# The experts' weight split moved out of the self-attention stage into 25 periods of the cross-attention

## Chip, cores and metric

One core of one Trainium2 chip runs the whole program. The metric is the device time of one execution in microseconds (us), smaller is better.

## What is computed

One block of a perceiver: 32 batch elements of 64 tokens, width 256, 16 heads of 16. Three layers stand behind one another, each added to its input: cross-attention to a context of 1601 rows per batch element, causal self-attention with a gate for each key, and a mixture of 8 experts of which each token takes two.

```python
x = x + xattn(layernorm(x), ctx, ctx, mask, Wq, bq, Wk, bk, Wv, bv)      # softmax(q k^T / 16) v over 1601 keys
x = x + attn(layernorm(x), ...)                                          # causal, attn * gate[key], then @ Wo
...
for e in range(E):                                                       # E = 8, F = 704
    h1 = x_rep @ w1[e].T
    a, g = jnp.split(h1, 2, axis=-1)
    he = jax.nn.silu(a) * g @ w2[e].T
    out = out + jnp.where((expert_ids == e)[:, None], he, 0)
```

All arrays are float32. The kernel multiplies with float16 pairs: a high part that is the rounded value, and a low part that is what the rounding lost.

## The kernel before

**Stages.** A lead-in (0 to about 74 us: layer norm, queries, keys and values of batch element 0), 31 periods of the cross-attention (about 74 to 1329 us), the self-attention stage, in which the last batch element's cross-attention is finished too (1329 to 1576 us), the router (to 1610 us) and the experts (to 1882 us). There is no scheduler at run time: what each engine does in a period, and in which order, stands in tables of step names written out in the file (`PE_ORDER`, `ACT_ORDER`, `POOL_ORDER`, `DVE_ORDER`, and `SELF_PE` to `SELF_SP` for the self-attention stage). Each engine runs its own list in order and waits on semaphores.

**A period.** In period b the attention of batch element b runs beside the projections of element b+1. On PE (TensorE), `S0`..`S12` are the transposed scores of 13 blocks of 128 keys, `W0`..`W12` the products of weights and values, `K0`..`K7` and `V0`..`V6` the projections of the next element, `M0`..`M15` scores whose maxima are wanted, two matmuls of 402 columns each. On ACT (ScalarE) `E` are two exponentials of 128x1024 (`pT` in float32, `ph` in float16), `KH` writes the high part of a key projection, `CH` that of the context. On POOL (GpSimd) `L` is `low_part`, which subtracts `ph` from `pT`, both in SBUF, into `pl`; `CL` does the same with the context, `ADD` adds a finished pair of elements to `x_all`, in every second period. On DVE (VectorE) `X0`..`X15` is `maxima`: the scores of `M` in PSUM plus the mask `mbias`, reduced to a maximum; `KL` is the low part of a key projection, `VH`, `VL` the two parts of a value projection, `N` the division by the row sums, `MP` the mask for two elements on.

**The banks.** `M(n+1)` writes the two PSUM banks that `X(n)` reads, so it waits for `X(n)`, and since PE runs in order, all of PE's list behind it waits too. `X(n+1)` waits for `M(n+1)`. Between `X(n)` and `X(n+1)` DVE thus has at least the length of an `M` without work of the maxima.

**SP (the DMA queue).** SP issues a period's transfers in this order: the context of b+2 (`cx`), queries (`qst`), twelve transfers of keys of the first half (`kst`, after `KL3`), mask and block queries (`msk`, `qm`), twelve of the second half (after `KL7`), and last the row that holds the maxima (`shift_queries`, `qst<-turned`). `S0` of the next period waits for that last one.

**Weights of the experts.** The 8 experts' weights are 24 pieces of 128x1408 float32. Each is loaded into `w_whole` (step `WL` on SP), its high part is made by ACT (`HI`, an activation with a scale), its low part by DVE (`LW`, a `scalar_tensor_tensor` that reads `w_whole` and the high part, both in SBUF), and both are stored to DRAM (`WS`). All 24 stand between the steps of the self-attention stage. The experts' stage loads them from there after the router.

**Self-attention stage.** `ZS`, `ZE`, `ZL`, `ZW` and `ZN` are the last element's `S`, `E`, `L`, `W` and `N`. `ST`, `N` make the layer norm's scale of a group of tiles (`newton_rsqrt`, some 14 small dependent DVE instructions), `XN` applies it, `X` turns tiles, `Q`, `K`, `V` project, `QH`, `QL`, `KH`, `KL`, `VV` keep them, `MX`, `RM`, `T`, `MC` find the maxima, `S`, `E`, `W`, `O` are the attention, `A`, `AC`, `WO`, `R` the output projection, `NU` and `XU` the next layer norm, `TU`, `CU`, `RT`, `RC` the router's products, `BO` adds a bias on POOL.

Of the kernel before, what the change touches and what calls it, by code (L numbers as in the profile page):

```python
# [137 lines left out]
SELF_PE = steps("ZS0 ZS1 ZS2 ZW0 ZS3 ZS4 ZW1 ZS5 ZW2 ZS6 ZW3 X0 X1 ZW4 ZS7 V0 V1 ZW5 ZS8 Q0 Q1 ZS9 ZW6 ZS10 ZW7 ZW8 V2 "  # L138
# [7 lines left out]
SELF_ACT = steps("ZE0 ZE1 ZE2 ZE3 ZE4 XN0 XN1 XN2 XN3 ZE5 XC0 XC1 XN4 ZE6 ZE7 ZE8 QH0 QH1 ZE9 ZE10 ZE11 ZE12 KH0 XN5 "  # L146
# [6 lines left out]
SELF_POOL = steps("ZL0 ZL1 ZL2 ZL3 ZL4 BO0 ZL5 ZL6 ZL7 ZL8 ZL9 ZL10 ZL11 ZL12 BO1 ZA0 BO2 HG0 BO3 HW0 PR0 HM0 VG0 VG1 "  # L153
                  "VG2 VG3 HG1 HW1 PR1 HM1 VG4 VG5 VG6 VG7")
SELF_DVE = steps("ZN0 ST0 ST1 ST2 ST3 ST4 N0 ST5 ST6 ST7 ST8 ST9 ST10 ST11 ST12 ST13 ST14 N1 VV0 HS0 VV1 HS1 QL0 QL1 "
# [1711 lines left out]
```

## Time and profile before

| | us |
|---|---|
| median of 3 runs | 1889.3 (1888.94 to 1891.74) |
| the profiled execution, its time | 1884.02 |
| its span, first to last instruction | 1882.2 |
| 31 periods of the cross-attention, one | 40.33 mostly, 40.5 on average |
| self-attention stage | 247 |
| router | 34 |
| experts | 272 |

The profiled execution lies 5.3 us under the median. PE is busy 92% of the span, DVE 74%, ACT and POOL 69% each; in the periods of the cross-attention PE is at 98 to 99%, in the self-attention stage at 82%.

### The profile page before, as it was taken

The page shows a single profiled execution, that of the slowest core. Times are in us where ns is not written, and L with a number is a line of the kernel's source. Part 1 is how long each engine was busy: PE and PEld are TensorE (multiplying, and loading weights), DVE is VectorE, ACT ScalarE, POOL GpSimd, SP SyncE. Part 2 cuts the span into 40 slices and gives each one's busy share as a digit, 9 for nine tenths or more (in the row PEclk, how much of TensorE's full clock was granted, in tenths as well). Part 3 has the DMA queues.
Part 4 walks back from the last instruction along what each step waited for, and adds up shares of the span by engine and source line. Part 5 has one row for each costly group of instructions (what it writes and reads, how often), then busy time and mean ns, then how long its engine had stood idle before and what let it go on. Part 6 is the DMA issues. An engine that isn't in the chain of part 4 may idle for free. (4 is left out here: it accounts for less than half of the span.)

```text
span 1882.2 us, 59167 instructions
## 1 busy us (share of the span) xinstructions
PE 1736.2 (92%) x24673; PEld 1146.0 (61%) x24673; DVE 1387.1 (74%) x3579; ACT 1307.0 (69%) x1610; POOL 1293.4 (69%) x669
## 2 busy tenths in 40 slices
PE   6899999999999999999999999999778993699996
PEld 3566666666666666666666666666534672588885
DVE  7788888888888888888888888788766566544443
ACT  5588788888878888878888878888664442233332
POOL 3488888898888888898898888888652100243442
PEclk9999999999999999999999999999898785799998
DMA  8544445444445544445554545554166674688884
GB/s 274 157 119 121 128 113 156 130 127 112 131 117 151 136 129 112 131 117 146 138 132 111 132 117 142 134 138 104 51 215 203 202 236 148 241 248 254 267 245 119
DMA packets 170923, 290.83 MB, mean 155 GB/s; under 512 B 56162, under 2 KB 138466, under 8 KB 170434
## 3 DMA queue, kind: packets, MB, share of 16 engines
q1 hardware_dynamic: 163170, 276.83, 50.6%
q0 software_dynamic: 7488, 10.23, 2.7%
q8 instruction: 196, 3.21, 0.7%
q14 instruction: 69, 0.57, 0.1%
HBM read 169.80 MB, written 33.16 MB: 108 GB/s over the span
## 5 line engine op out<-in xcount | busy, mean ns | idle before, releaser
L420 POOL TENSOR_TENSOR pl<-pT,ph 128x1024 f16<-128x1024 f32 x416 | 881.7, 2132 | 188.4 <-ACT ph L462 188.2
L679 DVE CUSTOM_DVE_ANT_0 junk<-ring,mbias 128x804 bf16<-128x804 f32 x496 | 491.5, 991 | 155.7 <-issue 150.1
L460 ACT ACTIVATE pT<-score,small 128x1024 f32<-128x1024 f32 (+1 forms) x416 | 464.5, 1117 | 68.0 <-PE score L485 34.0
L462 ACT ACTIVATE ph<-score,small 128x1024 f16<-128x1024 f32 (+1 forms) x416 | 464.5, 1117 | 0.0
L883 PE MATMUL ring<-cp,wkp 128*128 128x402 f16 x1536 | 309.0, 338 | 10.2 <-DVE kst L758 3.3
L894 PE MATMUL ring<-wvp,cp 128*128 128x256 f16 (+1 forms) x2496 | 306.3, 274 | 2.9 <-DVE v L664 1.7
L894 PEld LDWEIGHTS ring<-wvp,cp 128*128 128x128 f16 (+1 forms) x2496 | 233.7, 99 | 78.4 <-issue 21.8
L623 POOL TENSOR_TENSOR cp<-cx,cp 128x804 f16<-128x804 f32 x128 | 252.9, 1996 | 21.5 <-ACT cp L792 21.5
L800 ACT ACTIVATE kh<-ring,small 128x402 f16<-128x402 f32 x256 | 155.2, 606 | 154.9 <-PE ring L883 154.9
L908 PE MATMUL ring<-kh,qm 32*128 32x402 f16 x992 | 253.1, 334 | 4.9 <-DVE mx L679 0.3
L507 PE MATMUL o_acc<-v,pl 128*128 128x33 f16 (+1 forms) x3328 | 240.2, 178 | 0.0
L502 PE MATMUL o_acc<-v,ph 128*128 128x66 f16 x2912 | 219.7, 192 | 1.4 <-POOL pl L420 1.2
L883 PEld LDWEIGHTS ring<-cp,wkp 128*128 128x128 f16 x1536 | 131.9, 98 | 134.7 <-DVE v L664 25.8
L502 PEld LDWEIGHTS o_acc<-v,ph 128*128 128x128 f16 x2912 | 179.6, 97 | 54.8 <-issue 41.7
L507 PEld LDWEIGHTS o_acc<-v,pl 128*128 128x128 f16 (+1 forms) x3328 | 211.8, 96 | 1.6 <-issue 0.8
L485 PEld LDWEIGHTS score<-qst,kst 64*128 64x128 f16 x6656 | 156.3, 97 | 49.2 <-issue 1.1
L670 DVE SCALAR_TENSOR_TENSOR kl<-ring,small,kh 128x402 f16<-128x402 f32 x256 | 160.1, 634 | 21.5 <-ACT kh L800 16.9
L481 PE MATMUL score<-delta,mbias 64*128 64x512 bf16 (+1 forms) x832 | 163.3, 389 | 12.8 <-ACT ph L462 5.7
L655 DVE CAST v<-ring 128x512 f16<-128x512 f32 (+1 forms) x217 | 140.3, 652 | 44.7 <-PE ring L894 41.3
L485 PE MATMUL score<-qst,kst 64*128 64x64 f16 x6656 | 167.0, 191 | 0.0
L1488 POOL DMA_INDIRECT acc_d<-ys,to_row x39 | 63.1, 1617 | 144.9 <-DMA acc_d<-ys,to_row 72.1
L1755 PE MATMUL score<-xp,w1p 128*128 128x256 f16 (+1 forms) x1584 | 151.2, 254 | 5.4 <-DMA w1p<-wsp 5.0
(243 smaller groups left out, 2098.5 us busy)
## 6 DMA issues: line engine op xcount, KB each, us to landing
cx<-in_ctxT SPq DMA_DIRECT2D x32, 1601.0 KB, 6.7
w1p<-wsp SPq DMA_DIRECT2D x24, 1408.0 KB, 8.0
kst<-kh SPq DMA_DIRECT2D x256, 100.5 KB, 2.9
...
kst<-kh SPq DMA_DIRECT2D x256, 99.6 KB, 2.5
...
kst<-kl SPq DMA_DIRECT2D x128, 100.5 KB, 2.7
```

The lines of the kernel that those rows point to most:

```text
L420: pool.tensor_tensor(pl[:, u].rearrange("p h q -> p (h q)"), pT[:, u], ph[:, u].rearrange("p h q -> p (h q)"), ALU.subtract).then_inc(pl_r ...
L460: act.activation(pT[0:n, u].rearrange("k (h a q) -> k a h q", a=2, q=S), scored, ACT.Exp, bias=lift[0:n, 0:1], scale=SSCALE)
L462: act.activation(ph[0:n, u].rearrange("k h (a q) -> k a h q", a=2), scored, ACT.Exp, bias=lift[0:n, 0:1], scale=SSCALE).then_inc(exp_done, 1)
L481: pe.matmul(score[0:n, 2 * slot + side, :], mbias[part, j, rows], delta[part, :], start=True, stop=False, skip_group_check=True)
L485: mm = pe.matmul(score[0:n, 2 * slot + side, S * p:S * p + S], kst[j][part, p, rows], qst[part, j, p, :], start=False, stop=True, skip_gro ...
L502: pe.matmul(o_acc[:, at:at + 2 * PW], high, vv.rearrange("k z w -> k (z w)"), start=(kt == 0 and p == 0), stop=last, skip_group_check=True)
L507: mm = pe.matmul(o_acc[:, at:at + PW], low, vv[:, 0, :], start=False, stop=last, skip_group_check=True)
L623: pool.tensor_tensor(cp[:, j, 1, :, chunk(n)], cx[:, :, chunk(n)], cp[:, j, 0, :, chunk(n)], ALU.subtract).then_inc(cl_ready, 1)
L679: dve.tensor_tensor_reduce(junk[:, n % 2], made[:, :, 0:KW], mbias[:, j, 2 * KW * half:2 * KW * half + 2 * KW].rearrange("p (c k) -> p c k ...
L883: mm = pe.matmul(ring[:, bank, 0:KW], wkp[:, z, cc, P * t:P * t + P], cp[:, j, y, cc, chunk(c)], start=(cc == 0 and z == y), stop=(cc == D ...
L894: mm = pe.matmul(ring[0:n, bank, D * half:D * half + D], cp[:, j, z, cc, P * kt:P * kt + n], wvp[:, y, cc, :], start=(cc == 0 and z == y), ...
L908: mm = pe.matmul(to[:, c, 0:KW], qm[rows, j, t], kh[rows, t, chunk(2 * half + c)], start=True, stop=True)
```

## The change

The 24 pieces are split in the cross-attention. Period b (0 to 23) loads piece b and makes its high part on ACT as the last step of `ACT_ORDER`; period b+1 makes the low part on DVE in four slices of 352 columns (`LW0` to `LW3`, each where `DVE_ORDER` names it) and stores both. There is one buffer in place of two, over tiles of the lead-in that are no longer read (`xn`, `pack`, `bv`). The self-attention stage keeps all its other steps, in new orders on all engines, and its small tiles lie elsewhere. No arithmetic is changed.

```diff
+LPARTS = 4
+WSLICE = WP // LPARTS
...
-DVE_ORDER = steps("KL0 N KL1 KL2 VH0 VL0 KL3 X0 KL4 X1 X2 VH1 X3 VL1 X4 X5 KL5 X6 VH2 X7 VL2 X8 X9 KL6 X10 X11 KL7 X12 "
-                  "X13 VH3 X14 VL3 X15 SH VH4 SPR VL4 VH5 VH6 VL5 VL6 MP")
+DVE_ORDER = steps("KL0 N KL1 KL2 VH0 VL0 KL3 LW0 X0 KL4 X1 LW1 X2 VH1 X3 VL1 X4 X5 KL5 X6 VH2 X7 VL2 X8 LW2 X9 KL6 X10 "
+                  "LW3 X11 KL7 X12 X13 VH3 X14 VL3 X15 SH VH4 SPR VL4 VH5 VH6 VL5 VL6 MP")
...
-SELF_DVE = steps("ZN0 ST0 ST1 ST2 ST3 ST4 N0 ST5 ST6 ST7 ST8 ST9 ST10 ST11 ST12 ST13 ST14 N1 VV0 HS0 VV1 HS1 QL0 QL1 "
+SELF_DVE = steps("ST0 ST1 ST2 ST3 N0 ZN0 ST4 ST5 ST6 ST7 ST8 ST9 ST10 ST11 N1 VV0 HS0 VV1 ST12 ST13 HS1 ST14 VV2 QL0 "
...
+                    def load_whole(q):
+
+                        e, k = q // PIECES, q % PIECES
...
+                        after(sp, w_low, LPARTS * q)
+                        if k < DC:
+                            sp.dma_start(w_whole[:], a["w1T"][e, P * k:P * k + P]).then_inc(w_in, 16)
...
+                    def store_parts(q):
+
+                        sp.wait_ge(w_low, LPARTS * q + LPARTS)
+                        sp.dma_start(wsp[q // PIECES, q % PIECES], w_parts[:]).then_inc(w_out, 16)
...
+                        if 1 <= b <= E * PIECES:
+                            store_parts(b - 1)
+                        if b < E * PIECES:
+                            load_whole(b)
                         stack_keys(b + 1, 1 - j, 1)
...
+                            elif kind == "LW" and 1 <= b <= E * PIECES:
+                                cols = slice(WSLICE * n, WSLICE * n + WSLICE)
+                                dve.wait_ge(w_high, b)
+                                dve.scalar_tensor_tensor(w_parts[:, 1, cols], w_whole[:, cols], WSCALE, w_parts[:, 0, cols], ALU.mult, ALU.subtract).then_inc(w_low, 1)
...
+                            elif kind == "HI" and b < E * PIECES:
+                                act.wait_ge(w_in, 16 * (b + 1 + (b + 1) // PIECES))
+                                after(act, w_out, 16 * b)
+                                act.activation(w_parts[:, 0], w_whole[:], ACT.Copy, scale=WSCALE).then_inc(w_high, 1)
...
-                        elif kind == "LW":
-                            j = n % 2
-                            dve.wait_ge(w_high, n + 1)
-                            dve.scalar_tensor_tensor(w_parts[:, j, 1], w_whole[:, j], WSCALE, w_parts[:, j, 0], ALU.mult, ALU.subtract).then_inc(w_low, 1)
...
-                        elif kind == "HI":
```

The piece of DVE's list from `KL3` to `X2` in a period, before (`ISA junk,mx` is the maximum, `ISA mx` the read of its result):

```order
L670 SCALAR_TENSOR_TENSOR kl<-ring,small,kh 128x402
L678 MEMSET small 128x1
L679 ISA junk,mx<-ring,mbias 128x804
L679 ISA mx 128x1
L670 SCALAR_TENSOR_TENSOR kl<-ring,small,kh 128x402
L678 MEMSET small 128x1
L679 ISA junk,mx<-ring,mbias 128x804
L679 ISA mx 128x1
L678 MEMSET small 128x1
L679 ISA junk,mx<-ring,mbias 128x804
```

The same piece now:

```order
L699 SCALAR_TENSOR_TENSOR kl<-ring,small,kh 128x402
L755 SCALAR_TENSOR_TENSOR w_parts<-w_whole,w_parts 128x352
L707 MEMSET small 128x1
L708 ISA junk,mx<-ring,mbias 128x804
L708 ISA mx 128x1
L699 SCALAR_TENSOR_TENSOR kl<-ring,small,kh 128x402
L707 MEMSET small 128x1
L708 ISA junk,mx<-ring,mbias 128x804
L708 ISA mx 128x1
L755 SCALAR_TENSOR_TENSOR w_parts<-w_whole,w_parts 128x352
L707 MEMSET small 128x1
L708 ISA junk,mx<-ring,mbias 128x804
```

`LW0` stands ahead of `X0` and `LW1` ahead of `X2`; in the same way `LW2` stands ahead of `X9` and `LW3` ahead of `X11`. All four read two tiles in SBUF.

SP's list in the middle of a period, before, from the end of the first half's keys:

```order
L548 DMA kst<-kl 32x2x804
L527 DMA msk<-in_mask 64x1601 x2
L532 DMA qm<-qm_d 128x256
L548 DMA kst<-kh 32x2x797 x2
L548 DMA kst<-kl 32x2x797
```

The same place now:

```order
L549 DMA kst<-kl 32x2x804
L528 DMA msk<-in_mask 64x1601 x2
L533 DMA qm<-qm_d 128x256
L572 DMA wsp<-w_parts 128x2816
L562 DMA w_whole<-in_w1T 128x1408
L549 DMA kst<-kh 32x2x797 x2
```

The store of one piece and the load of the next stand between `qm` and the second half's keys; the store waits for `LW3`.

The head of DVE's list in the self-attention stage, before (the first eight rows end the step `ZN0`):

```order
L442 TENSOR_TENSOR osum<-o_acc,rs 64x112
L443 TENSOR_TENSOR o_acc<-o_acc,rs 64x7x16
L442 TENSOR_TENSOR osum<-o_acc,rs 64x112
L443 TENSOR_TENSOR o_acc<-o_acc,rs 64x7x16
L448 TENSOR_TENSOR att<-osum,o_acc 64x7x16
L449 TENSOR_SCALAR att<-o_acc,rs 64x16
L448 TENSOR_TENSOR att<-osum,o_acc 64x7x16
L449 TENSOR_SCALAR att<-o_acc,rs 64x16
L1094 BN_STATS st_x<-x_all 128x6 x5
L1101 BN_AGGR mv_70<-st_x 128x2 x4
```

And now:

```order
L1112 BN_STATS st_x<-x_all 128x6 x4
L1119 BN_AGGR mv_72<-st_x 128x2 x4
L231 TENSOR_SCALAR ln_ve<-mv_72 128x4
L232 TENSOR_SCALAR ln_t<-ln_ve 128x4
L233 TENSOR_SCALAR ln_ve<-ln_ve 128x4
```

The first layer norm's scales (`N0`) no longer stand behind `ZN0`, and on ACT `XN0` now stands behind two steps `ZE` where five stood before.

## Rows read from the trace of the kernel before

**Rows 1.** Busy us by stage (x instructions): PE, PEld, DVE, ACT, POOL; clock, DMA share, GB/s

```profile
164.00:1290.00 1126.00, 1109.71 (x17095) 698.99 (x17095) 923.20 (x2387) 940.07 (x1053) 988.55 (x486) 1.00 0.48 128
1329.00:1576.00 247.00, 201.39 (x2962) 135.23 (x2958) 160.69 (x423) 131.83 (x182) 66.75 (x40) 0.83 0.59 191
```

**Rows 2.** Timeline of one period (start us, us, engine, instruction): DVE, then PE

```profile
931.03 0.64 DVE L670 SCALAR_TENSOR_TENSOR kl<-ring,small,kh 128x402 f16<-128x402 f32 x1
932.46 0.99 DVE L679 CUSTOM_DVE_ANT_0 junk<-ring,mbias 128x804 bf16<-128x804 f32 x1 [0.79 <-issue]
...
934.09 0.99 DVE L679 CUSTOM_DVE_ANT_0 junk<-ring,mbias 128x804 bf16<-128x804 f32 x1
...
935.71 0.99 DVE L679 CUSTOM_DVE_ANT_0 junk<-ring,mbias 128x804 bf16<-128x804 f32 x1 [0.61 <-issue]
...
946.97 0.99 DVE L679 CUSTOM_DVE_ANT_0 junk<-ring,mbias 128x804 bf16<-128x804 f32 x1
...
948.70 0.99 DVE L679 CUSTOM_DVE_ANT_0 junk<-ring,mbias 128x804 bf16<-128x804 f32 x1 [0.73 <-issue]
...
950.31 0.99 DVE L679 CUSTOM_DVE_ANT_0 junk<-ring,mbias 128x804 bf16<-128x804 f32 x1
...
952.01 0.99 DVE L679 CUSTOM_DVE_ANT_0 junk<-ring,mbias 128x804 bf16<-128x804 f32 x1 [0.70 <-issue]
...
933.52 0.51 PE L908 MATMUL ring<-kh,qm 32*128 32x402 f16 x2
```

**Rows 3.** Timeline of POOL in that period, and in one with ADD (first row)

```profile
890.89 4.22 POOL L420 TENSOR_TENSOR pl<-pT,ph 128x1024 f16<-128x1024 f32 x2
...
928.46 4.25 POOL L420 TENSOR_TENSOR pl<-pT,ph 128x1024 f16<-128x1024 f32 x2
...
935.85 4.22 POOL L420 TENSOR_TENSOR pl<-pT,ph 128x1024 f16<-128x1024 f32 x2 [0.63 <-ACT ph L462]
...
945.22 6.33 POOL L420 TENSOR_TENSOR pl<-pT,ph 128x1024 f16<-128x1024 f32 x3
952.45 2.13 POOL L420 TENSOR_TENSOR pl<-pT,ph 128x1024 f16<-128x1024 f32 x1 [0.90 <-ACT ph L462]
```

**Rows 4.** Timeline of POOL and DVE where both ran in SBUF

```profile
1333.80 10.46 POOL L420 TENSOR_TENSOR pl<-pT,ph 128x1024 f16<-128x1024 f32 x5 [5.62 <-ACT ph L462]
...
1342.23 2.05 DVE L239 TENSOR_TENSOR ln_t<-ln_t,ln_ve 128x4 f32<-128x4 f32 x1
...
1453.02 2.35 POOL L1068 TENSOR_TENSOR hd<-hd,lnb 128x1024 f32<-128x1024 f32 x1
...
1453.23 3.63 DVE L1159 SCALAR_TENSOR_TENSOR w_parts<-w_whole,w_parts 128x1408 f16<-128x1408 f32 x1 [0.51 <-ACT w_parts L1247]
```

**Rows 5.** Instructions of the tiles w_parts and ln_t: count, ns min/median/max

```profile
L1247 ACT ACTIVATE w_parts<-w_whole x24: 1360/1368/1389, 1378.5 to 1574.1; 128x1408 f16<-128x1408 f32 x24
L1159 DVE SCALAR_TENSOR_TENSOR w_parts<-w_whole,w_parts x24: 1600/1618/3628, 1382.5 to 1575.5; 128x1408 f16<-128x1408 f32 x24
...
L239 DVE TENSOR_TENSOR ln_t<-ln_t,ln_ve x33: 161/164/2054, 7.4 to 1567.8; 128x4 f32<-128x4 f32 x21, 128x8 f32<-128x8 f32 x9, 128x12 f32<-128x12 f32 x3
```

**Rows 6.** Timeline of ACT at the end of a period

```profile
924.54 0.60 ACT L800 ACTIVATE kh<-ring,small 128x402 f16<-128x402 f32 x1 [4.43 <-PE ring L883]
```

**Rows 7.** Timeline of SP there, and landing of the tile turned

```profile
921.77 0.60 SPq L563 DMA_DIRECT2D qst<-turned  x1
...
DMA to landing us min/median/max: 1.8/1.9/3.4
```

**Rows 8.** PE's waits in the self-attention stage: us in total, times, longest

```profile
PE ring L1366 <- ACT kst L1238: 6.2, 1, 6.2
...
PE ring L1304 <- ACT xn L1197: 3.7, 1, 3.7
...
PE ring L1304 <- DVE klo L1113: 2.3, 1, 2.3
PE o_acc L1349 <- DVE ao L1165: 2.0, 1, 2.0
```

More of the change, by code:

```diff
@@ L137 @@
 HT = TILES // 2
[L138 removed]
[7 rows of a table removed]
[L146 removed]
[6 rows of a table removed]
[L153 to L155 removed]
[8 rows of a table removed]
[L164 removed]
[3 rows of a table removed]
+SELF_PE = steps("ZS0 ZS1 ZS2 ZS3 X0 ZW0 ZW1 X1 ZS4 V0 V1 ZS5 ZW2 Q0 V2 V3 ZS6 Q1 ZS7 ZW3 ZW4 ZW5 K0 K1 ZW6 ZS8 ZS9 X2 "
[7 rows of a table added]
+SELF_ACT = steps("ZE0 ZE1 XN0 XN1 XN2 XN3 ZE2 XC0 XC1 ZE3 ZE4 XN4 XN5 XN6 XN7 QH0 ZE5 QH1 ZE6 ZE7 KH0 KH1 ZE8 XN8 XN9 "
[5 rows of a table added]
+SELF_POOL = steps("ZL0 ZL1 BO0 ZL2 ZL3 ZL4 BO1 ZL5 ZL6 ZL7 ZL8 BO2 ZL9 ZL10 ZL11 ZL12 HG0 ZA0 HW0 PR0 BO3 HM0 VG0 VG1 "
+                  "VG2 VG3 HG1 HW1 PR1 HM1 VG4 VG5 VG6 VG7")
+SELF_DVE = steps("ST0 ST1 ST2 ST3 N0 ZN0 ST4 ST5 ST6 ST7 ST8 ST9 ST10 ST11 N1 VV0 HS0 VV1 ST12 ST13 HS1 ST14 VV2 QL0 "
[7 rows of a table added]
+SELF_SP = steps("RO0 SQ0 SK0 SK1 SH0 RO1 SQ1 SH1 SH2 SK2 SH3 SH4 SQ2 SK3 SH5 SH6 SH7 SH8 SQ3 SH9 AS0 SH10 XS0 AS1 SH11 "
+                "XS1 SH12 SH13 SH14 AS2 XS2 SH15 AS3 XS3")
 SELF_USES = [use for use in SELF_PE if use[0] in ("X", "Q", "K", "V", "T", "A", "TU")]
@@ L197, in program @@
         ident = sb("ident", [P, P])
-        xn = sb("xn", [P, 4, D])
         ln_st = sb("ln_st", [P, TILES, 6])
@@ L250, in mark @@
                 return -(-nc.sbuf_base // 32) * 32
+            at_first = mark()
+            pack = sb1("pack", [P, PACK])
+            wk, wv, wq = (pack[:, DC * D * n:DC * D * n + DC * D].rearrange("p (c d) -> p c d", c=DC) for n in range(3))
+            bk, bq, sel_q = (pack[:, 3 * DC * D + DC * n:3 * DC * D + DC * n + DC] for n in range(3))
+            bv = sb1("bv", [P, D])
+            w_whole = nc.alloc_sbuf_tensor_at("w_whole", [P, WP], F32, offset=at_spent)
+            w_parts = nc.alloc_sbuf_tensor_at("w_parts", [P, 2, WP], F16, offset=at_spent + 4 * WP)
             at_consts = mark()
+            assert at_spent + 8 * WP <= at_consts
             cx = sb1("cx", [P, DC, NKP])
@@ L258, in program @@
             at_soon = mark()
-            pack = sb1("pack", [P, PACK])
-            wk, wv, wq = (pack[:, DC * D * n:DC * D * n + DC * D].rearrange("p (c d) -> p c d", c=DC) for n in range(3))
-            bk, bq, sel_q = (pack[:, 3 * DC * D + DC * n:3 * DC * D + DC * n + DC] for n in range(3))
-            bv = sb1("bv", [P, D])
             cp = sb1("cp", [P, 2, 2, DC, NKP], F16)
@@ L332, in room @@
                 return place
-            consts, late, soon, last = (room(at, end) for at, end in ((at_consts, at_keys), (at_keys, at_soon),
-                                                                      (at_soon, at_mbias + 2 * NKP), (at_last, at_end)))
+            first, consts, late, soon, last = (room(at, end) for at, end in ((at_first, at_consts), (at_consts, at_keys), (at_keys, at_soon),
+                                                                             (at_soon, at_mbias + 2 * NKP), (at_last, at_end)))
             wq2, wk2, wo2 = (consts(n, [P, DC, D]) for n in ("wq2", "wk2", "wo2"))
@@ L345, in program @@
             turner = consts("turner", [P, P])
-            mv1, mvh, mv2 = (soon(n, [P, TILES, 2]) for n in ("mv1", "mvh", "mv2"))
-            inv1, invh, inv2 = (soon(n, [P, TILES]) for n in ("inv1", "invh", "inv2"))
-            off1, offh, off2 = (soon(n, [P, TILES]) for n in ("off1", "offh", "off2"))
-            st_x, st_h, st_y = (soon(n, [P, TILES, 6]) for n in ("st_x", "st_h", "st_y"))
+            mv1, mvh, mv2 = (first(n, [P, TILES, 2]) for n in ("mv1", "mvh", "mv2"))
+            inv1, invh, inv2 = (first(n, [P, TILES]) for n in ("inv1", "invh", "inv2"))
+            off1, offh, off2 = (first(n, [P, TILES]) for n in ("off1", "offh", "off2"))
+            st_x, st_h, st_y = (first(n, [P, TILES, 6]) for n in ("st_x", "st_h", "st_y"))
             xt = soon("xt", [P, 2, DC, CH])
@@ L355, in program @@
             hd = soon("hd", [P, TILES, DP])
-            drift, pre, gate = soon("drift", [P, 2, TILES]), soon("pre", [P, TILES, GW]), soon("gate", [P, 2, TILES])
-            top2 = soon("top2", [P, 2, STRIP])
-            mtc = soon("mtc", [STRIP, 4, P], F16)
-            rs2 = soon("rs2", [P, H])
+            drift, pre, gate = first("drift", [P, 2, TILES]), first("pre", [P, TILES, GW]), first("gate", [P, 2, TILES])
+            top2 = first("top2", [P, 2, STRIP])
+            mtc = first("mtc", [STRIP, 4, P], F16)
+            rs2 = first("rs2", [P, H])
             pT2 = late("pT2", [P, 2, H, S])
@@ L377, in program @@
             first2_in, consts2_in, rows2_in = sem("first2_in"), sem("consts2_in"), sem("rows2_in")
-            w_in, w_out = [sem(f"w_whole_in{j}") for j in range(2)], [sem(f"w_parts_out{j}") for j in range(2)]
+            w_in, w_out = sem("w_whole_in"), sem("w_parts_out")
             w_high, w_low = sem("w_high_parts"), sem("w_low_parts")
@@ L1242, in _ @@
                             act.activation(xt2[:, n % 2], bank("TU", n)[:, 0:D].rearrange("p (c k) -> p c k", c=DC), ACT.Copy).then_inc(yt_ready, 1)
-                        elif kind == "HI":
-                            e, k, j = n // PIECES, n % PIECES, n % 2
-                            act.wait_ge(w_in[j], 16 * sum(1 if q % PIECES < DC else 2 for q in range(j, n + 1, 2)))
-                            after(act, w_out[j], 16 * (n // 2))
-                            act.activation(w_parts[:, j, 0], w_whole[:, j], ACT.Copy, scale=WSCALE).then_inc(w_high, 1)
                 @block.tensor
@@ L1456, in load @@
                                          whole[:, z, (FT - 1) * D:WP].rearrange("(r h) f -> r h f", h=2)).then_inc(w2_in[j], 16)
-                    for j in range(2):
-                        sp.wait_ge(w_out[j], 16 * (E * PIECES // 2))
                     sp.wait_ge(te_ready, 1)
```

35 lines of the change are left out of this document (14 added, 21 removed), and 41 rows, old and new, of tables (SELF_ACT, SELF_DVE, SELF_PE, SELF_SP).

## The prediction, made before the changed kernel had run

> **What bounds the kernel now.** I read the windows by stage first [rows 1]. In the cross-attention's periods PE is busy 1109.7 of 1126 us, and the granted clock is 1.00: PE sets the length of a period, and whatever stops PE there is paid in full. In the self-attention stage PE is busy 201.4 of 247 us, so 45.6 us are idle, and the clock is at 0.83. There the order of the steps and the waits between engines set the length.
>
> Next the timeline of DVE in one period, and with it one row of PE [rows 2]. `X0` ends at 933.45 and PE's next `M` starts at 933.52: PE takes it up within 0.07 us, so a late `X` is a late PE. Between two maxima DVE has a gap. It is 0.79 us ahead of `X0` (from the end of `KL3`, 931.67, to 932.46), 0.63 ahead of `X2`, 0.74 ahead of `X9`, 0.71 ahead of `X11`. These are the four places of the slices.
>
> Then POOL's timeline in the same period [rows 3], since POOL is busy 988.6 of 1126 us: at nearly every moment a `low_part` of 2.1 us is under way. And last the places where a DVE instruction that reads two SBUF tiles met a POOL instruction [rows 4]. The low part of a whole piece takes 1.61 us [rows 5]. The one issued at 1453.23 took 3.63: POOL's product of 1453.02 ran to 1455.37, and from there it is 1.5 us to its end. At the head of the self-attention stage POOL ran five `low_part` from 1333.80 to 1344.26, 2.09 us each [rows 4]. A DVE product of two small SBUF tiles, whose median is 0.16 us [rows 5], took 2.05 there, from 1342.23 to 1344.28, the end of the fifth. So such an instruction waits for the rest of the POOL instruction that is under way.
>
> **The change, part by part.**
>
> *High parts in the periods.* 24 activations of 1.37 us [rows 5] at the end of ACT's list. ACT sat idle 4.43 us ahead of the next `KH0` [rows 6]. The cover is three times the need; I cost it at nothing. Uncovered it would be 24 × 1.37 = 33 us, but for that the gap would have to vanish.
>
> *Low parts in the periods.* A slice has a quarter of 1408 columns. A quarter of 1.61 is 0.40; with a fixed part that doesn't shrink I take 0.45, an estimate. Alone it would fit in each of the four gaps. With POOL's instruction under way it doesn't.
> - `LW0` comes at 931.67; POOL's second `low_part` ends at 928.46 + 4.25 = 932.71. The slice ends at 933.16, so `X0` is 0.70 late. In periods with `ADD` POOL is later: `KL3` ends at 891.35 and POOL's instruction at 890.89 + 2.11 = 893.00 [rows 3], so the slice ends at 893.45. `X0`, 0.79 behind `KL3` before, stood at 892.14: 1.31 late.
> - `LW1` came, as things stood, at 935.08, and POOL is free until 935.85. 0.70 late it comes at 935.78, still just ahead. 1.31 late it comes at 936.39, behind it, and waits to 937.96; the slice ends at 938.41, and `X2` is 2.70 late instead of 1.31. The next `low_part` can't shift with it, since its exponential hangs on scores that stand ahead of the late `M` on PE.
> - `LW2` comes at 947.96, when three `low_part` run back to back from 945.22; the second ends at 949.44. The slice ends at 949.89 and `X9` is 1.19 late. From `S5` on all engines have shifted together, so I take this phase as unchanged.
> - `LW3` comes at 951.30 + 1.19 = 952.49 and POOL's next starts at 952.45. That is a toss: ahead of it nothing is lost, behind it the slice ends at 954.58 + 0.45 = 955.03 and `X11` (952.01) is 3.02 late, 1.83 more.
>
> A period thus loses (0.70 + 2.70)/2 + 1.19 = 2.89 us if `LW3` wins and 4.72 if it loses. I take the middle, 3.8: 24 × 3.8 = **+91 us**. If each slice cost only what it costs in the phase of before, it would be (0.70 + 1.31)/2 + 1.19 = 2.2, or 53 us. If `LW1` and `LW3` always lost it would be 2.70 + 1.19 + 1.83 = 5.72, or 137 us. Behind a late `X` wait PE's `M`, then all of PE's list, and with it ACT's exponentials.
>
> The row of 1453.23 shows this wait for one form beside one POOL instruction. The Trainium skill, "SBUF — State Buffer", section "Who interferes with whom", makes it general: a DVE instruction with two SBUF inputs and a GpSimd instruction that reads SBUF exclude each other, and the later one waits to the end. By the rule every slice meets `low_part` as worked out here; without it, if the row were an exception, the sum would be that of the fast rival below.
>
> *SP.* Per piece one store and one or two loads stand between `qm` and the second half's keys; an issue takes SP 0.60 us [rows 7], so 1.2 to 1.8 in all. The store waits for `LW3`; the keys wait for `KL7`, which follows `LW3` by `X11` and itself, 0.99 + 0.64 us. So the issues fit, to 0.2 us, under a wait that is there anyway. 1.44 MB more per period goes ahead of the keys and the row of the maxima, whose issue at 921.77 is followed by `S0` at 924.38, 2.6 us on, with a landing of 1.9 [rows 7]. Slack: some 0.5 us. I cost it at nothing; the bound is 0.5 us late in each period, 12 us.
>
> *Self-attention stage.* It loses 24 × 1.37 us of ACT and 24 × 1.62 us of DVE, of which only what PE waited for counts. PE's waits there [rows 8]: 3.7 us for `XN0`, behind `N0`, which now starts without `ZN0` ahead and meets two `low_part` instead of five; 2.3 for a low part of keys, behind a piece on ACT and one on DVE; 2.0 for `O`, behind the 3.63 us piece; 6.2 at the tail for `XU12`, which the new order covers with ten steps `TU` and `RT`. That is 14.2. The last piece, 1.62 us, stood behind everything else. Smaller waits behind the pieces I put at 4, an estimate: **−20 us**. Bounds: 8 (only the head, the last piece and a little), and 45.6, all of PE's idle time.
>
> **The sum.** 1884.0 + 91 − 20 = 1955 us for an execution like the profiled one. That one lies 5.3 us under the median of the runs, so I forecast **1960 us**.
>
> **The rivals.**
> - *No cascade*: each slice loses only its own rest, 2.2 us a period. For it: the phases are those of the rows. Against it: two of the four margins are under 0.1 us. 1884 + 53 − 20 + 5 = 1922 us.
> - *All margins lost*: 5.7 us a period: 1884 + 137 − 20 + 5 = 2006 us. For it: once PE stalls, phases drift, and POOL is busy 88% of the time.
> - *Faster*: the slices run in DVE's gaps without meeting POOL, because a slice gets in ahead of a `low_part` or the wait doesn't apply to it. Then only the stage's gain is left: 1884 − 20 + 5 = 1869 us. The point from which it decides is 20/24 = 0.83 us lost in a period. Against it: `LW2` alone comes in the middle of three POOL instructions and loses 1.19.
> - *The queue in place of the lock*: no wait on DVE, but the row of the maxima lands up to 1 us late behind 1.44 MB, 24 us: 1884 + 24 − 20 + 5 = 1893 us, no change.
>
> **How the numbers follow.** Cascade in part (2.9 to 4.7 us a period, 1938 to 1982 us): 0.50. No cascade: 0.17. All lost: 0.17. Faster: 0.12. Queue: 0.04. The range that holds 8 in 10 takes in the first three, from 1910 (no cascade, and 12 us more gained in the stage) to 2012; above and below stand the fast case, the queue and the far end with a late queue. A measurement of this kernel can tell about 0.2% from no change. Faster by over that 0.12, within 0.03, slower 0.85.
>
> **What the changed kernel's profile would show.** Right: low-part slices of 0.45 to 0.5 us when alone, and means well above 1 us, each long one ending 0.4 to 0.5 behind the end of a POOL `low_part`; periods of 43 to 45 us with PE's share near 92%; PE waiting for DVE's maxima at the `M`s of `X0`, `X2`, `X9`, `X11`; a self-attention stage of some 227 us. Wrong: slices all at 0.5 us and periods near 40.4 us; or periods longer with the slices short, and PE waiting ahead of `S0`. The prediction fails most easily by the phases: a shift of 0.1 us moves a margin of `LW1` or `LW3`, worth 1.4 to 1.8 us a period.

## The result, and the profile after

The changed kernel took 1905.5, 1908.8 and, in the profiled execution, 1917.0 us. A fourth execution took 2099.0 us at a mean granted clock of 0.74, against 0.95 to 0.96 in these three, and is left out of every comparison. The time is **1.0114 times** that of the kernel before, with a 95% interval of 1.007 to 1.0158: 1.1% slower, some 21 us. I had forecast 1960 us, 71 us more, with 8 chances in 10 between 1910 and 2012. The direction was right. The median, 1908.8 us, lies just below that range, and the size is less than half of the forecast.

The windows of the changed kernel by stage come first: the 24 periods that hold the experts' weights, then the self-attention stage.

```profile
113.22:1158.49 1045.27, 987.00 (x14761) 616.30 (x14760) 908.88 (x2161) 847.45 (x935) 873.09 (x421) 0.97 0.54 152
1403.37:1613.48 210.11, 189.53 (x2932) 128.32 (x2951) 120.87 (x397) 100.94 (x158) 62.80 (x40) 0.86 0.22 64
```

The same stretches of the kernel before:

```profile
114.14:1085.57 971.43, 959.41 (x14762) 603.72 (x14760) 797.84 (x2065) 813.25 (x912) 855.17 (x421) 1.00 0.48 129
1330.80:1578.19 247.39, 201.12 (x2951) 135.07 (x2951) 160.63 (x421) 131.83 (x182) 66.75 (x40) 0.83 0.59 191
```

The periods took 73.8 us more, the stage 37.3 less, the other stages 3.5 less: +33.0 us between the two spans (1882.2 and 1915.2). The 73.8 us have two parts. PE's idle time (first number less the second) rose from 12.0 to 58.3 us, by 46.3. And PE's busy time rose by 27.6 us for the same instructions, because the granted clock fell from 1.00 to 0.97. Only the first part was in my sum.

PE's waits in those periods (us in total, times, longest), and the slices:

```profile
PE ring L945 <- DVE mx L708: 44.2, 48, 1.2
PE score L482 <- issue: 4.9, 11, 0.7
```

```profile
L755 DVE SCALAR_TENSOR_TENSOR w_parts<-w_whole,w_parts x96: 519/1515/2444, 122.0 to 1145.1; 128x352 f16<-128x352 f32 x96
```

PE waits for DVE's maxima, twice in each of 24 periods, 44.2 us in all. By place, a slice took 1.51 us at `LW0` (1.87 to 2.17 in seven of the twelve periods with `ADD`), 0.52 at `LW1` in 17 periods and 2.1 to 2.4 in those same seven, 1.94 at `LW2`, and 0.52 in all 24 at `LW3`. In the other five periods with `ADD` PE had waited 0.56 to 0.92 us ahead of `S0`; there `LW0` took 1.51 us and `LW1` 0.52.

The dearest period, 501.30 to 548.00, on DVE's timeline and then POOL's:

```profile
508.06 0.64 DVE L699 SCALAR_TENSOR_TENSOR kl<-ring,small,kh 128x402 f16<-128x402 f32 x1
508.61 2.17 DVE L755 SCALAR_TENSOR_TENSOR w_parts<-w_whole,w_parts 128x352 f16<-128x352 f32 x1
510.71 0.98 DVE L708 CUSTOM_DVE_ANT_0 junk<-ring,mbias 128x804 bf16<-128x804 f32 x1
...
513.28 2.10 DVE L755 SCALAR_TENSOR_TENSOR w_parts<-w_whole,w_parts 128x352 f16<-128x352 f32 x1
515.32 0.98 DVE L708 CUSTOM_DVE_ANT_0 junk<-ring,mbias 128x804 bf16<-128x804 f32 x1
...
528.76 1.94 DVE L755 SCALAR_TENSOR_TENSOR w_parts<-w_whole,w_parts 128x352 f16<-128x352 f32 x1
```

```profile
508.25 6.75 POOL L421 TENSOR_TENSOR pl<-pT,ph 128x1024 f16<-128x1024 f32 x3
```

POOL ran three `low_part` from 508.25 to 515.00. `LW0`, come at 508.61, ends at 510.78, and `LW1`, come at 513.28, ends at 515.38, 0.4 behind POOL's third. This is the wait for POOL's instruction, which I call the lock, and the cascade (a slice delayed by one wait meets POOL's next instruction and waits again), as worked out from [rows 2 to 4]. What followed on PE is in the windows of the next 10 us (us, PE busy, granted clock):

```profile
509.30:511.30 2.00, 1.27 (x36) 1.00 1.01 416
511.30:513.30 2.00, 1.54 (x22) 0.70 1.14 265
513.30:515.30 2.00, 2.00 (x22) 0.50 0.80 174
515.30:517.30 2.00, 2.00 (x11) 0.50 0.60 158
517.30:519.30 2.00, 2.00 (x35) 0.60 0.77 156
```

PE stood idle for 1.2 us, and behind that the granted clock went from 2.4 to 1.2 GHz for about 7 us. Once PE runs again it is busy all the time (2.00 of 2.00), at half speed: the loss shows as busy time. Three periods, from cheap to dear:

```profile
203.15:244.92 41.77, 39.92 (x617) 1.00 0.56 160
244.92:288.68 43.76, 41.29 (x617) 0.96 0.54 152
501.30:548.00 46.70, 44.20 (x617) 0.89 0.50 142
```

A period of before took 40.3 us at the least. In 12 of the 24 changed periods the clock is below 1.00; in none of before. These 12 hold 14 falls: seven behind a stall at `LW0` of 1.05 to 1.19 us, seven behind the one at `LW2`, which is 1.03 to 1.04 us long in every period.

In the self-attention stage the waits of [rows 8] are gone but for the one at the head (`XN0`), which is 3.6 us in place of 3.7:

```profile
PE ring L1313 <- ACT xn L1211: 4.0, 2, 3.6
PE score L482 <- ACT ph L463: 3.0, 3, 1.8
...
PE ring L1325 <- DVE hd L1152: 2.4, 1, 2.4
```

### The profile page after: what moved, and what is told of

It is laid out like the page before. It is cut to its first block and busy times, and to the rows that moved or that the text cites. A ratio compares the mean times of both kernels' runs of the same rounds, so it can differ in the third digit from the quotient of the medians.

```text
span 1915.2 us, 59222 instructions
## 1 busy us (share of the span) xinstructions
PE 1749.8 (91%) x24654; PEld 1151.3 (60%) x24673; DVE 1459.0 (76%) x3651; ACT 1311.4 (68%) x1610; POOL 1306.7 (68%) x669
## 5 line engine op out<-in xcount | busy, mean ns | idle before, releaser
L421 POOL TENSOR_TENSOR pl<-pT,ph 128x1024 f16<-128x1024 f32 x416 | 899.2, 2172 | 249.1 <-ACT ph L463 247.9
L931 PE MATMUL ring<-wvp,cp 128*128 128x256 f16 (+1 forms) x2496 | 317.4, 280 | 2.9 <-DVE v L693 1.7
L945 PE MATMUL ring<-kh,qm 32*128 32x402 f16 x992 | 260.2, 342 | 48.2 <-DVE mx L708 44.2
L931 PEld LDWEIGHTS ring<-wvp,cp 128*128 128x128 f16 (+1 forms) x2496 | 238.7, 101 | 87.0 <-issue 25.3
L699 DVE SCALAR_TENSOR_TENSOR kl<-ring,small,kh 128x402 f16<-128x402 f32 x256 | 160.0, 632 | 21.5 <-ACT kh L833 18.9
```

Of the source, the lines that this page charges most:

```text
L421: pool.tensor_tensor(pl[:, u].rearrange("p h q -> p (h q)"), pT[:, u], ph[:, u].rearrange("p h q -> p (h q)"), ALU.subtract).then_inc(pl_r ...
L931: mm = pe.matmul(ring[0:n, bank, D * half:D * half + D], cp[:, j, z, cc, P * kt:P * kt + n], wvp[:, y, cc, :], start=(cc == 0 and z == y), ...
L945: mm = pe.matmul(to[:, c, 0:KW], qm[rows, j, t], kh[rows, t, chunk(2 * half + c)], start=True, stop=True)
```

## The experiments

All ratios are to the kernel before, run on the same chip. Edits are against the changed kernel where nothing else is said. "24 periods" is the stretch of the first windows row above, found in each trace by its first and last mask instruction.

**One SBUF input per slice.**

```diff
-dve.scalar_tensor_tensor(w_parts[:, 1, cols], w_whole[:, cols], WSCALE, w_parts[:, 0, cols], ALU.mult, ALU.subtract)
+dve.tensor_reduce(w_parts[:, 1, cols], w_whole[:, cols].unsqueeze(2), AX.X, ALU.max)
```

> Changed: each low-part slice is a reduction over an axis of length 1 that reads one SBUF tile (352 columns of the whole weights) instead of two, and writes the same 352 columns; the stored low parts are then copies of the weights. Everything else, order and transfers too, is as in the changed kernel. Theory A (an instruction of VectorE with two SBUF inputs excludes GpSimd's low_part): slices of 0.5 us in all 96 places, periods of about 40.3 to 41.4 us, clock 1.00, total about 1840 to 1870 us. Rival B (the work and the queue position of four more instructions per period, whatever they read): the 0.52 us of each slice stays, and the periods of 41.8 to 46.7 us stay with it, total 1900 to 1915 us. Rival C (the store and load of the pieces on the queues disturb other transfers): also unchanged, 1900 to 1915 us.

Measured: 1844.3 us, ratio 0.9761 (0.9744 to 0.9777). Its slices, its 24 periods and one period:

```profile
L755 DVE TENSOR_REDUCE w_parts<-w_whole x96: 509/515/518, 121.6 to 1074.8; 128x352 f16<-128x352 f32 x96
```

```profile
113.12:1088.19 975.07, 958.03 (x14762) 604.14 (x14760) 838.99 (x2161) 842.20 (x935) 855.81 (x421) 1.00 0.57 163
```

```profile
154.45:194.78 40.33, 40.04 (x617) 1.00 0.58 165
```

The same count, order, columns and transfers cost 3.6 us over before in place of 73.8, and a period can be 40.33 us as before. So the work in the periods, ACT's high parts and the traffic are hidden; what costs is the second SBUF input. The Trainium skill, "SBUF — State Buffer", section "Who interferes with whom", says that a DVE instruction with two SBUF inputs contends with a GpSimd instruction that reads SBUF, and that one with at most one does not, if it is outside the perf modes that use two ports. The minimum and maximum here (509 and 518 ns, against 519 and 2444 with two inputs) agree. One input alone is no safe sign: at the head of the self-attention stage of before, beside the five `low_part` of [rows 4], a `tensor_scalar` with a single small SBUF input, whose median is 0.17 us, took 2.05:

```profile
1338.07 2.05 DVE L234 TENSOR_SCALAR ln_ve<-ln_ve 128x4 f32<-128x4 f32 x1
```

**16 columns in place of 352**, from the second period on (most of the low parts left out):

```diff
-cols = slice(WSLICE * n, WSLICE * n + WSLICE)
+cols = slice(WSLICE * n, WSLICE * n + (WSLICE if b < 2 else 16))
```

> Changed: from the second of the 24 periods on each low-part slice handles 16 columns instead of 352, in the same form with two SBUF inputs; most of the low parts are left out. Theory A (the slice waits for GpSimd's instruction under way): LW0 and LW2 still take 1.1 to 1.6 us, LW1 and LW3 0.15 us outside the cascades; periods of 41 to 42.5 us, total 1860 to 1890 us. Rival B (the number of columns that VectorE handles sets the cost): slices of 0.15 us in all places, periods of 40.3 to 40.5 us, total 1840 to 1850 us.

Measured: 1872.4 us, ratio 0.9897 (0.9841 to 0.9952). Slices of 1.17 to 1.81 us at `LW0` and 1.60 at `LW2`, 0.17 at the others; the cheapest period 41.08 us. 22 times less data shortened the long slices by only 0.35 us: the rest is waiting. This kernel has the same operation as the changed one, so it also rules out that the first experiment was fast by its other operation alone.

**Place by place.** Two inputs at one place only, the other three slices as in the first experiment:

```diff
+if n in (0,):      # the other kernel: (2,)
     dve.scalar_tensor_tensor(...)
+else:
+    dve.tensor_reduce(...)
```

> Changed: only the first slice of each period (LW0, ahead of X0) has two SBUF inputs; the other three are reductions with one SBUF input, so three quarters of the low parts are copies of the weights. If the terms per place are as I worked them out, LW0 costs 0.7 us a period and 1.3 in the eight ADD periods, 20 to 25 us in all over the 1844 us with no slice of two inputs. If the granted clock's fall is set off by each late maximum by itself, the price is up to double that: 35 to 45 us. If LW0 causes nothing by itself (its delay is made up before S0's end), the total is within 5 us of 1844 us.

> Changed: only the third slice of each period (LW2, ahead of X9) has two SBUF inputs; the other three have one. As worked out, LW2 costs 1.19 us a period, 29 us in all over 1844 us: about 1873 us. With a fall of the granted clock behind the stalls 1880 to 1890 us. If only LW0 and the cascade made the cost: within 5 us of 1844 us.

Measured: `LW0` alone 0.9867 (0.9817 to 0.9917), `LW2` alone 0.9973 (0.9949 to 0.9997; nine executions between 1874 and 1896 us, the profiled one the shortest). A cheap period and one with `ADD` of the first, then a cheap one of the second; then PE's waits of each:

```profile
196.52:237.26 40.74, 39.91 (x617) 1.00 0.57 164
237.26:278.65 41.39, 39.92 (x617) 1.00 0.55 161
```

```profile
156.50:197.87 41.37, 40.05 (x617) 1.00 0.56 161
```

```profile
PE ring L948 <- DVE mx L708: 19.0, 24, 1.2
```

```profile
PE ring L948 <- DVE mx L708: 25.2, 25, 1.1
```

`LW0` costs 0.41 us (1.06 with `ADD`), `LW2` 1.04. They add: 40.33 + 0.41 + 1.04 = 41.78, the cheapest period of the changed kernel is 41.77, and 19.0 + 25.2 = 44.2 is just what PE waited there. Of the periods, seven and six fell below clock 1.00; the six of `LW2` alone stand behind stalls of 1.04 us. That the total of `LW0` alone, 21.5 us above the first experiment, lies in the 20 to 25 us that I expected is luck: in its 24 periods PE was idle 15.9 us longer, less than my term, and busy 11.8 us longer, which my term did not have.

**Delay without the lock.** One SBUF input, but more of it:

```diff
+k = (4, 3, 4, 1)[n]
+dve.tensor_reduce(w_parts[:, 1, cols], w_whole[:, 0:WSLICE * k].rearrange("p (c k) -> p c k", k=k), AX.X, ALU.max)
```

> Changed: the slices read one SBUF tile each, but 1408, 1056, 1408 and 352 columns of it (maximum over 4, 3, 4 and 1 columns), so that VectorE is held 1.6, 1.25, 1.6 and 0.5 us at the four places, near the means of the changed kernel (1.69, 1.02, 1.94, 0.52), with no exclusion of GpSimd; the low parts are not computed. Theory A' (the price is only the delay of the maxima behind each slice, plus the clock's fall after the stalls): periods of 42.5 to 44.5 us, granted clock 0.96 to 0.98 in them, total 1895 to 1920 us. Rival E (what costs is what the exclusion does to GpSimd and to the small instructions beside it, not the delay): periods of 40.3 to 41.5 us, total 1845 to 1865 us.

Measured: 1879.0 us, ratio 0.995 (0.9925 to 0.9975), between the two theories. A typical period:

```profile
156.80:198.57 41.77, 40.00 (x617) 1.00 0.56 159
```

The cheap period of the changed kernel was 41.77 too, so a delay of this size makes those 1.44 us without any lock. That the two agree to 0.01 us is partly chance: the two long stalls of this period are 0.64 and 0.71 us, those of the changed kernel 0.54 and 1.04. But only two of 24 periods had a fall of the clock. PE's stalls at the two places here were 0.6 to 0.8 us long; in the changed kernel 0.5 to 0.7 and 1.0 behind `LW0` and `LW2`, and 1.05 to 1.19 behind `LW0` in the `ADD` periods with a cascade. So I held VectorE 0.5 us longer at `LW0` (and halved the fourth slice):

```diff
+if n == 3: cols = slice(WP - WSLICE // 2, WP)
 dve.tensor_reduce(...)                      # as above
+if n == 0:
+    dve.tensor_reduce(w_parts[:, 1, WSLICE * 3:WP - WSLICE // 2], w_whole[:, 0:WSLICE].rearrange("p (c k) -> p c k", k=2), AX.X, ALU.max)
```

> Changed against e8: at LW0 VectorE is held about 0.5 us longer (a second instruction with one SBUF input), 2.1 us in all, as long as the slice of the changed kernel takes in its ADD periods; LW3 is shorter by half. No instruction has two SBUF inputs and the low parts are not computed. Theory A'' (in the changed kernel the granted clock fell behind PE's longer stalls, about 1.1 us at one place, and not through the exclusion itself): PE idle per period about 2.3 us, the clock at 0.5 for some microseconds behind many of the stalls near offset 9, mean clock of the 24 periods 0.94 to 0.98, PE busy time 975 to 1000 us there, periods 42.3 us at the least, total 1900 to 1935 us. Rival F (the clock fell because of the exclusion, or by chance): clock 1.00 as with e8, PE busy 962 us, total 1888 to 1895 us.

Measured: 1902.7 us, ratio 1.0088 (1.0068 to 1.0107). The 24 periods and two neighbours, with and without a fall:

```profile
113.88:1147.87 1033.99, 976.52 (x14762) 610.26 (x14760) 908.71 (x2185) 846.05 (x935) 856.45 (x421) 0.98 0.54 154
```

```profile
544.73:588.57 43.84, 41.42 (x617) 0.96 0.54 152
588.57:630.76 42.19, 39.99 (x617) 1.00 0.54 158
```

Now PE's stall behind `LW0` is 1.06 to 1.22 us long in all 24 periods and the clock falls behind it in 12, though no slice has two SBUF inputs. Against the kernel with the shorter delay PE's idle time rose by 9.3 us (48.2 to 57.5) and its busy time by 14.3 (962.2 to 976.5). Together that is 23.6 us, and the medians of all executions differ by 23.7. The fall belongs to the stall on PE, not to the lock.

**Both kernels once more**, unchanged:

> The kernel before once more, for how far its stages differ from one profiled execution to the next: periods of 40.33 us at the least, the 24 periods 970 to 974 us; self-attention stage 235 to 250 us, with the granted clock in it between 0.80 and 0.90.

> The changed kernel once more: cheapest periods 41.77 us, the 24 periods 1030 to 1050 us, a length that differs by where the clock fell; self-attention stage 199 to 211 us.

Measured: 1890.5 and 1918.5 us, one execution each. Self-attention took 254.9 us (before, clock 0.78, both outside what I had expected) and 207.0 (changed), the 24 periods 972.8 and 1047.0. This trace of the changed kernel has ten cascades where the first has seven, and three of them stand in periods at full clock. In a fourth, PE stalled 1.35 us at the cascade and the clock fell right behind that: the period took 47.7 us, the dearest of all. Two of its periods with a cascade:

```profile
157.12:200.69 43.57, 40.01 (x617) 1.00 0.53 152
941.38:985.16 43.78, 41.29 (x617) 0.96 0.53 152
```

**No cascade.** `LW1` alone with one input:

```diff
+if n in (0, 2, 3):
     dve.scalar_tensor_tensor(...)
+else:
+    dve.tensor_reduce(...)
```

> Changed: the second slice of each period (LW1) alone is a reduction with one SBUF input; LW0, LW2 and LW3 keep two inputs (a quarter of the low parts are copies). With LW1 out of it no slice can meet the low_part that an earlier slice has pushed back. If the cascade costs nothing in PE's idle time (the additive reading of e5 and e6): the 24 periods keep about 58 us of PE idle, total 1900 to 1920 us. If the cascade costs what I worked out or near it (2 us and more in the seven periods that have it, with falls of the clock behind it): 15 to 30 us less, 1880 to 1900 us.

Measured: 1908.8 us, ratio 1.0109 (1.0076 to 1.0142); PE waits 44.4 us for the maxima. Two of its `ADD` periods:

```profile
928.20:970.60 42.40, 39.92 (x617) 1.00 0.55 157
498.44:542.23 43.79, 41.30 (x617) 0.96 0.53 152
```

Read against the pair above, this prices the cascade; the totals (1.0109 and 1.0114) cannot. At full clock it costs 43.57 − 42.40 = 1.17 us, 1.08 of it idle time (3.56 against 2.48). Where the clock has just fallen behind `LW0`'s stall it costs nothing, 43.78 against 43.79: in those periods PE does not stall for `X2`, since at half speed it is late itself. In the first trace of the changed kernel all seven cascades stood in such periods.

**The slices elsewhere.** Three slices (352, 704, 352 columns), ahead of `X2`, `X5` and `X11`. All work is done in this kernel and in the next three.

```diff
-LPARTS = 4
-WSLICE = WP // LPARTS
+LPARTS = 3
+WCUTS = (0, WP // 4, 3 * WP // 4, WP)
-KL3 LW0 X0 KL4 X1 LW1 X2 VH1 X3 VL1 X4 X5 KL5 X6 VH2 X7 VL2 X8 LW2 X9 KL6 X10 LW3 X11
+KL3 X0 KL4 X1 LW0 X2 VH1 X3 VL1 X4 LW1 X5 KL5 X6 VH2 X7 VL2 X8 X9 KL6 X10 LW2 X11
```

> Changed: three slices in place of four (352, 704 and 352 columns), and placed ahead of X2, X5 and X11, where the timeline of before shows GpSimd between two low_part instructions or close to the end of one. All work is done. Theory A (the place against GpSimd's instructions sets the price): the slices take 0.5 to 1.0 us each with seldom a wait, periods of 40.4 to 41.5 us at a granted clock near 1.00, total 1850 to 1875 us. Rival B (the sum of VectorE's work sets it): periods as before the move, total 1900 us and more. Rival D (GpSimd's timeline moves against VectorE's once the slices are there, so that they meet again): total 1880 to 1900 us.

Measured: **1842.5 us**, ratio 0.9758 (0.974 to 0.9775): 46 us faster than before, and by the two ratios some 67 us faster than the changed kernel.

```profile
L755 DVE SCALAR_TENSOR_TENSOR w_parts<-w_whole,w_parts x72: 564/595/890, 125.8 to 1079.2; 128x352 f16<-128x352 f32 x48, 128x704 f16<-128x704 f32 x24
```

```profile
114.64:1092.55 977.91, 958.50 (x14762) 604.22 (x14760) 840.49 (x2138) 843.19 (x935) 855.90 (x421) 1.00 0.57 163
```

Little of the waiting is left: 352 columns, 0.52 us alone, take 0.59 to 0.82 ahead of `X2` and 0.57 ahead of `X11`. The cheapest period is 40.45 us, the 24 periods cost 6.5 us over before, and the clock stays at 1.00 in all of them. Then four slices, ahead of `X2`, `X5`, `X11` and `X13`:

```diff
-KL3 X0 KL4 X1 LW0 X2 ... X4 LW1 X5 ... X10 LW2 X11 KL7 X12 X13
+KL3 X0 KL4 X1 LW0 X2 ... X4 LW1 X5 ... X10 LW2 X11 KL7 X12 LW3 X13
```

> Changed: four slices of 352 columns as in the changed kernel, with two SBUF inputs, but placed ahead of X2, X5, X11 and X13. Full computation. If the place decides and not the number of slices: slices of 0.52 us, shortest periods of 40.4 to 40.5 us, total 1838 to 1850 us. If it was the smaller number of instructions: shortest periods near 41 us, total 1855 to 1870 us.

Measured: 1928.5 us, ratio 1.0216 (1.0164 to 1.0268). I had not expected this at all: no slice takes over 0.71 us, and the kernel is slower than the changed one. Slices, PE's waits, and SP's timeline of one period:

```profile
L755 DVE SCALAR_TENSOR_TENSOR w_parts<-w_whole,w_parts x96: 519/553/711, 124.5 to 1164.4; 128x352 f16<-128x352 f32 x96
```

```profile
PE score L482 <- issue: 58.7, 21, 4.3
```

```profile
986.94 0.35 SPq L572 DMA_DIRECT2D wsp<-w_parts  x1
987.33 0.43 SPq L564 DMA_DIRECT2D w_whole<-in_w2T  x1
987.81 1.05 SPq L566 DMA_DIRECT2D w_whole<-in_w2T  x1
988.96 1.38 SPq L549 DMA_DIRECT2D kst<-kh  x2
...
997.72 0.60 SPq L588 DMA_DIRECT2D qst<-turned  x1
```

PE now waits ahead of `S0`, 58.7 us in all. SP's store waits for the last slice, behind it stand the load, the key stack and the shift of the queries, 10.8 us from the store's issue to the shift's, and `S0` starts at 999.90, 2.2 us behind the shift's issue. With the last slice behind `KL7`, nothing on SP is hidden under the wait for `KL7` any more. The clock is in this price too: against the kernel with three slices the 24 periods took 84.3 us more, 55.1 of them idle time of PE and 29.2 busy time, with the clock below 1.00 in 20 periods. Three kernels test the reading. The kernel with three slices, with its last slice ahead of `X13`:

```diff
-LW2 X11 KL7 X12 X13
+X11 KL7 X12 LW2 X13
```

> Changed against e4: the last of the three slices stands ahead of X13 instead of X11. Slices without a wait for GpSimd expected. If SP decides (its store of the parts waits for the last slice, and 13 more transfers with the rest of the stacked keys and the shift of the queries stand behind it): store near offset 32 to 37, PE waits before the scores at the head of periods, 40 us and more in the 24 periods, total 1900 to 1935 us. If e10's loss came from its fourth slice: 1838 to 1850 us.

Measured: 1932.1 us, ratio 1.0238 (1.0188 to 1.0289), 59.1 us of waits ahead of `S0`. And the kernel with four slices, with its fourth slice back ahead of `X11`:

```diff
-LW2 X11 KL7 X12 LW3 X13
+LW2 LW3 X11 KL7 X12 X13
```

> Changed against e10: the fourth slice stands right behind the third, ahead of X11, so four slices with the last one's end near offset 28.5. If SP decides: total 1840 to 1860 us (a little over e4 for the longer stretch ahead of X11). If the number of slices decides: 1900 us and more.

Measured: 1853.5 us, ratio 0.9823 (0.978 to 0.9867), 4.2 us of those waits. The place of the last slice decides, not the number. Behind the store the load is late too, and ScalarE waited for it in both slow kernels, 30.8 and 29.8 us in all. To part the two, the kernel of 1932.1 us with a high part that does not wait for the load (VectorE waits for it ahead of its first slice):

```diff
+dve.wait_ge(w_in, 16 * (b + b // PIECES))      # ahead of a slice
...
+if b < 1:
     act.wait_ge(w_in, 16 * (b + 1 + (b + 1) // PIECES))
-act.activation(w_parts[:, 0], w_whole[:], ACT.Copy, scale=WSCALE)
+act.activation(w_parts[:, 0], w_whole[:] if b < 1 else w_parts[:, 0], ACT.Copy, scale=WSCALE if b < 1 else 1.0)
```

> Changed against e11 (last slice ahead of X13): from the second piece on ScalarE's step HI copies w_parts in place and does not wait for w_whole to land; VectorE waits for that before the first slice instead, where it has long landed. The stored parts are not those of the reference. It tells apart the two things that are late behind the store: if SP's queue (key stack and shift, so PE waits before the scores) makes the loss, HI starts without a wait and the total stays at 1915 to 1940 us, with 50 us and more of PE waiting before the scores. If the late load that holds up HI and with it ScalarE makes the loss, the total falls to 1840 to 1870 us.

Measured: 1938.2 us, ratio 1.0251 (1.0182 to 1.0321). ScalarE waits no more, and PE does as before:

```profile
PE score L482 <- issue: 54.9, 20, 4.3
```

So the waits ahead of `S0` are those of SP's queue, not of ScalarE's wait for the load. Last, two slices of 704 columns ahead of `X2` and `X5`, with all work done:

```diff
-LPARTS = 3
-WCUTS = (0, WP // 4, 3 * WP // 4, WP)
+LPARTS = 2
+WCUTS = (0, WP // 2, WP)
-LW2 X11 KL7 X12 X13
+X11 KL7 X12 X13
```

> Changed against e4: two slices of 704 columns, ahead of X2 and X5, so that VectorE is done near offset 17 and SP's store waits for nothing. Full computation. If both limits (GpSimd's instruction under way, SP's store) are understood: slices of 0.9 to 1.1 us, periods of 40.3 to 40.7 us, total 1836 to 1848 us. If 704 columns ahead of X2 run into GpSimd or make X2 late: periods of 41 us and more, total 1855 to 1875 us.

Measured: 1841.3 us, ratio 0.9784 (0.9726 to 0.9842), not to be told from the kernel with three slices.

**The self-attention stage in the old order**, without the pieces in it:

```diff
-SELF_PE, SELF_ACT, SELF_POOL, SELF_DVE, SELF_SP of the changed kernel
+the tables of the kernel before, with WL, WS, LW and HI taken out
```

> Changed: the stage of self-attention takes the order tables of the kernel before, with the steps of the experts' weights taken out of them (they stay in the 24 periods of cross-attention). Theory A (most of the 37 us that the stage lost came with the pieces' work itself, the reorder gave the rest): the stage takes 215 to 235 us, total 1912 to 1930 us. Rival B (the reorder brought nearly all of it): stage 240 to 247 us, total about 1940 us. Rival C (the pieces alone did it): stage about 210 us, total 1908 us.

Measured: 1937.3 us, ratio 1.0274 (1.0228 to 1.032), above the 1912 to 1930 us that I had expected with a stage of this length. The stage, beside that of the second execution of before:

```profile
1395.07:1629.36 234.29, 201.62 (x2951) 134.31 (x2951) 121.74 (x396) 101.49 (x158) 62.63 (x40) 0.82 0.19 57
```

```profile
1332.55:1587.49 254.94, 211.32 (x2951) 143.38 (x2951) 160.62 (x421) 132.05 (x182) 66.76 (x40) 0.78 0.57 186
```

Taking the pieces out lowered PE's idle time from 46.3 and 43.6 us (the two traces of before) to 32.7, and the new order from there to 20.6 and 17.8 (the two traces of the changed kernel): a gain from each. The 15 traces of kernels with the new order have stages of 199.1 to 210.2 us with PE busy 180.8 to 192.7 us, 187.3 on average; in the three with the old order PE is busy 201.1 to 211.3 us, 204.7 on average, for the same instructions. So the new order also sees more of the full clock, some 17 us of busy time. Why one execution keeps it longer than another I cannot say.

## Why the prediction was right in direction and wrong in size

The mechanism, slices that wait for POOL's instruction and make `X` and so PE late, was right. Two steps of the sum failed. The path of delays that I drew on from `LW2` was wrong: `LW3` never met a `low_part`, so its 22 us were not there, and the cascade at `LW1`, 16.7 us of the sum, was rarer than I had it and cost nothing in this trace. And the clock had no term, though its falls cost 27.6 us. Step by step:

- *The lock.* Right: the first two experiments leave no other reading, and rows show it in each long slice.
- *`LW0` and `LW2`.* Right in mechanism, a little large: 0.70 (1.31 with `ADD`) and 1.19 us forecast, 0.41 (1.06) and 1.04 measured. In PE's waits 24.1 and 28.6 us forecast, 19.0 and 25.2 measured. The rows show where it went: a slice ended 0.38 us behind the end of POOL's instruction, where I had 0.45 (`LW1` above: 515.38 and 515.00), and the maximum starts 0.07 us ahead of the slice's recorded end (510.71 and 510.78). So `X0` was 0.57 us late in the cheap periods and PE stalled 0.54 us for it, and `X9`, by `LW2` alone, 1.06.
- *The cascade at `LW1`.* It occurs, in seven and ten periods where I had twelve: in the other periods with `ADD` PE had waited ahead of `S0`, and `LW0` was short. The size was near (1.39 us forecast, 1.17 measured at full clock), but in the first trace it cost nothing, since the clock had fallen in each such period. 16.7 us of the sum, none measured there; the second trace has four that cost something.
- *`LW3`.* This is the step that failed outright: "a toss", of which I took half, 22 us. The slice took 0.52 us in all 48 periods of two traces, so it always got in ahead of POOL, and it was POOL's instruction that took longer, 2.33 us in place of 2.13. In the dearest period:

```profile
533.15 0.52 DVE L755 SCALAR_TENSOR_TENSOR w_parts<-w_whole,w_parts 128x352 f16<-128x352 f32 x1
533.32 2.33 POOL L421 TENSOR_TENSOR pl<-pT,ph 128x1024 f16<-128x1024 f32 x1 [0.64 <-ACT ph L463]
```

By my own rows it came 0.04 us behind `low_part`'s start; with a delay of 1.04 us in place of 1.19 it comes 0.11 ahead. The kernel with two inputs at `LW2` alone bears this out: its fourth slice comes 28.02 us behind the start of a cheap period, 1.05 later than with no two-input slice (26.97), and the `low_part` stays at 28.19. So this error follows from the one of 0.15 us at `LW2`.
- *What replaced them.* PE's idle time grew by 46.3 us for 91 forecast. The fall of the granted clock, which my sum did not have, added 27.6 us of busy time, so that by luck 73.8 looks nearer to 91 than the reasoning was.
- *High parts at nothing.* Right, by the first experiment.
- *SP and the queue at nothing, bound 12 us.* Right for this kernel (waits ahead of `S0`, those behind the mask included, of 7.2 and 5.6 us in its two traces, 2.5 and 3.9 in those of before), but the bound was far off in its reason. I read the margin under `KL7`'s wait as 0.2 us and then bounded its loss by the landing of one transfer. The two kernels with the last slice ahead of `X13` show the price past it: over 80 us against the kernel with three slices, clock included.
- *Self-attention, −20 us.* It lost 37.3 us of length in the first pair of traces, 47.9 in the second. The idle time fell by 25.7 and 25.8, near the sum, though not by its terms: of the 3.7 us for `XN0` only 0.1 came. `N0` met two `low_part`, as I had it, and two of its small instructions took 2.04 and 2.05 us. The rest is PE's busy time at the better clock (11.6 and 22.1 us). The 24 periods and this stage both lacked a term for the clock, with opposite signs, and so the two omissions hide each other in the total.
- *The rivals.* "No cascade" (1922 us, chance 0.17) was nearest in time, and for a partly different reason: no wait at `LW3` and no cascade that cost anything, but falls of the clock, which it did not have. The fast rival's condition, under 0.83 us a period, does not hold for these places; at other places it does (three slices ahead of `X2`, `X5` and `X11`: 6.5 us in 24 periods, 0.27 in each).
